# A third buffer for transposed features, and the selection of half 1 between the first gram products

## What is computed

```python
e = jnp.stack([tbl_0[ids[:, 0]], ..., tbl_26[ids[:, 26]]], axis=1)      # 2048 x 27 x 128
interactions = jnp.einsum('bfd,bgd->bfg', e, e).reshape(B, F * F)
x = interactions[:, TRIL_IDX]                                           # 351 pairs
z = jnp.concatenate([bottom_mlp_out, x], axis=1)
h = jnp.concatenate([z, bottom_mlp_out], axis=1)
h = jnp.maximum(h @ W_top1 + b_top1, 0.0)                               # 607 x 512
h = jnp.maximum(h @ W_top2 + b_top2, 0.0)                               # 512 x 256
y = h @ W_top3                                                          # 256 x 1
```

## Time and profile before

| | us |
|---|---|
| timed, median of three (lowest, highest) | 381.1 (380.89, 382.53) |
| profiled execution, span | 633.3 |
| TensorE matmul busy in it | 402.0 |
| GpSimd busy | 262.1 |
| VectorE busy | 254.0 |
| ScalarE busy | 144.4 |

### The profile page before, as it was taken

How to read it: one execution, slowest core, us unless ns; L and a number is a source line. 1 busy time by engine, 2 the same in 40 slices (tenths; PEclk the granted TensorE clock), 3 DMA queues, 4 the chain that set the end, 5 groups by cost and what they waited for, 6 DMA issues and landing times.

```text
span 633.3 us, 10256 instructions
## 1 busy us (share of the span) xinstructions
PE 402.0 (63%) x4321; PEld 374.0 (59%) x4321; DVE 254.0 (40%) x341; ACT 144.4 (23%) x268; POOL 262.1 (41%) x283
## 2 busy tenths in 40 slices
PE   2207655492738928298465956469392892839997
PEld 2206543492727918197464955469381992829986
DVE  3117955191315704074040921338040560407422
ACT  3204722020302213112311123012130221311521
POOL 6761447317370364505463073712646045550010
PEclk9999967597668969599595996769776896959999
DMA  8812652114221232114121241211321132211021
GB/s 200 174 50 77 175 167 77 52 28 135 55 55 40 64 104 65 41 40 128 35 75 28 45 134 47 61 39 36 127 64 53 36 81 84 64 40 39 9 61 9
DMA packets 44889, 45.76 MB, mean 72 GB/s; under 512 B 32720, under 2 KB 35558, under 8 KB 43948
## 3 DMA queue, kind: packets, MB, share of 16 engines
q1 hardware_dynamic: 33646, 26.52, 16.3%
q0 software_dynamic: 8896, 17.89, 10.9%
q10 hardware_dynamic: 2302, 0.70, 0.5%
HBM read 39.52 MB, written 5.55 MB: 71 GB/s over the span
## 4 chain that ended last, share of the span: by engine, by line
PE 50%; issue 20%; another core or an unknown queue 18%; ACT 5%; DVE 4%; DMA 2%; SPq 0%; ACTq 0%; DVEq 0%
PE work L389 21%; PE gram L416 16%; PE work L401 3%; PE work L442 2%; PE work L443 2%; PE work L444 2%; DVE onehot L536 2%; ACT embT L506 2%; ACT embT L675 2%; DMA inter<-in_tbl 1%; PE work L470 1%; DVE tab_lo L521 1%; DMA misc<-in_bottom 1%; PE work L459 1%
## 5 line engine op out<-in xcount | busy, mean ns | idle before, releaser
L359 POOL DMA_INDIRECT emb<-in_tbl,ids_all x272 | 258.2, 949 | 304.9 <-PE work L401 217.7
L536 DVE TENSOR_TENSOR onehot<-ids_bc,row_idf 125x1024 fp32r<-125x1024 int32 (+2 forms) x232 | 199.4, 921 | 94.0 <-PE work L389 60.9
L416 PE MATMUL gram<-embT 128*54 128x52 f32 x2048 | 110.3, 264 | 161.7 <-issue 134.6
L389 PE MATMUL work<-onehot,tab_hi 125*128 125x256 f32 x672 | 172.8, 296 | 51.2 <-DVE onehot L536 26.0
L416 PEld LDWEIGHTS gram<-embT 128*54 128x54 f32 x2048 | 93.9, 179 | 181.5 <-issue 164.2
L389 PE MATMUL work<-onehot,tab_lo 125*128 125x256 f32 x672 | 169.2, 291 | 0.0
L389 PEld LDWEIGHTS work<-onehot,tab_hi 125*128 125x128 f32 x672 | 133.8, 199 | 57.0 <-DVE onehot L536 32.4
L389 PEld LDWEIGHTS work<-onehot,tab_lo 125*128 125x128 f32 x672 | 134.3, 200 | 0.0
L675 ACT COPY embT<-work 128x512 f32<-128x512 f32 (+1 forms) x41 | 30.4, 795 | 163.5 <-PE work L389 98.9
L569 DVE SCALAR_TENSOR_TENSOR x_lo<-work,x_hi 128x512 fp32r<-128x512 f32 x16 | 11.0, 691 | 103.9 <-ACT x_hi L708 72.6
L683 ACT COPY inter<-gram 118x416 f32<-118x416 f32 x64 | 32.3, 506 | 66.5 <-remote 33.6
(11 more groups left out here) (56 smaller groups left out, 220.9 us busy)
## 6 DMA issues: line engine op xcount, KB each, us to landing
ids_bc<-in_sel_ids SPq DMA_DIRECT2D x7, 1280.0 KB
grams<-inter SPq DMA_DIRECT2D x64, 84.5 KB
emb<-in_tbl,ids_all POOLq DMA_INDIRECT x272
misc<-in_tbl SPq DMA_DIRECT2D x3, 448.0 KB
inter<-in_tbl SPq DMA_DIRECT2D x3, 448.0 KB
ids_bc<-in_sel_ids SPq DMA_DIRECT2D x4, 256.0 KB, 5.2
misc<-in_bottom SPq DMA_DIRECT2D x8, 128.0 KB
raw_hi<-in_tbl SPq DMA_DIRECT2D x1, 560.0 KB
```

Of the source, the lines that this page charges most:

```text
L359: pool.indirect_dma_start(out=emb[:, t % TILE_SLOTS, f, :], out_offset=None, in_=gather_tables[f], in_offset=bass.IndirectOffsetOnAxis(ap= ...
L389: mm = nc.tensor.matmul(out, part[0:k, CHUNK_AT[f] + c, :], onehot[0:k, at % RING, i * HALF:(i + 1) * HALF], start=(c == 0 and i % 2 == 0 ...
L416: last = nc.tensor.matmul(gram[side * SIDE:side * SIDE + TWO * NF, n % 2, q, 0:COLS], two.rearrange("d s f -> d (s f)"), two[:, :, 0:NG], ...
L536: nc.vector.tensor_tensor(onehot[0:k, at % RING, 0:width], ids_bc[0:k, four[0]:four[-1] + 1, :].rearrange("p i n -> p (i n)"), row_idf[0:k ...
```

## The change

- **A third slot.** embT_third, in the place of x_hi, x_lo and h2, holds tile 2; tile 3 uses slot 0. So the selection of half 1 can be copied (in two halves of a copy, one for each tile) while tile 1's slot is still in use.
- **Order of halves 0 and 1.** In half 0 the transposes of tile 0 come one set earlier where they can, and those of tile 1 behind sets 4 and 5, all copied by ScalarE. Then products 0, set 0 of half 1, products 1, transposes of tile 2, sets 1 and 2, products 2, bottom rows of half 0, transposes of tile 3, mlp1 of half 0, products 3, bottom rows of half 1. From half 2 on the order is that of before.
- **Weights.** They are all loaded by SyncE, after the last split of a table, into the place where their rest part will stand; ScalarE rounds them, VectorE subtracts in place, behind the one-hot 12 of half 1. On ScalarE the roundings stand behind the copies of tile 2.
- **Ids** for the selection come in a load for each set with a semaphore each. The row of ones sits directly under the pairs; VectorE fills 32 rows with ones before the packs of half 0 are loaded, and SyncE waits for that.

```diff
-    ONES = -(-PAIR_ROWS[-1] // QS) * QS
+    ONES = PAIR_ROWS[-1]
-        return range(j - 1, NGR if j == len(TWOS) - 1 else j) if 0 < j <= NGR else range(0)
+        return range(0)
+
+    FIRST_ROWS = [[], [(0, 0)], [(0, 1), (0, 2)], [(0, 3), (0, 4)], [(1, 0), (1, 1)], [(1, 2), (1, 3), (1, 4)]]
...
+    for j in range(len(TWOS)):
+        take_select(0, j)
+        for t, g in FIRST_ROWS[j]:
+            take_rows(t, [g])
+    take_gram(0)
+    take_gram(1)
+    take_select(1, 0)
+    take_rows(2)
+    take_select(1, 1)
+    take_select(1, 2)
+    take_gram(2)
+    take("bottom", 0)
+    take_rows(3)
+    take_gram(3)
+    take_mlp(0, "mlp1")
+    take("bottom", 1)
...
+        with nc.sbuf_tensor("embT_third", [P, P, NF], F32) as embT_third:
+            pass
+        with (nc.sbuf_tensor("raw_x", [P, 2, M1 + 2, HALF], F32), nc.sbuf_tensor("raw_h2", [P, M2, HALF], F32), nc.sbuf_tensor("raw_w1", [P, 2, CH + 1, H1], F32) as raw_w1,
+              nc.sbuf_tensor("raw_w2", [P, 2, M1, H2], F32) as raw_w2):
+            pass
...
-        w1_bot = [packed[:, 0:2, :].rearrange("p c n -> p (c n)"), h2[:, :, :].rearrange("p m n -> p (m n)")]
-        w1_raw = [stage[3][:, c * H1:(c + 1) * H1] for c in range(2)] + [w1_bot[1]]
-        w2_raw = stage[2][:, 0:M1 * H2]
+
+        def tile_embT(t):
+            return embT_third if t == 2 else embT[:, 0 if t == 3 else t % 2, :, :]
...
-            raw_last = max(n for n, to in enumerate(STAGE_OF) if to > 1)
-            sp.wait_ge(table_hi, raw_last + 1)
-            sp.wait_ge(table_lo, SPLIT_BY[raw_last])
-            for c in range(2):
-                sp.dma_start(w1_raw[c], w_top1[D + c * P:D + (c + 1) * P, :]).then_inc(w1_loaded[c], 16)
-            sp.dma_start(w2_raw.rearrange("p (c n) -> p c n", n=H2), w_top2.rearrange("(c p) n -> p c n", p=P)).then_inc(w2_loaded, 16)
-            sp.wait_ge(table_hi, NSEL)
-            sp.wait_ge(table_lo, len(PIECES))
-            sp.dma_start(bot[:, :, :], bottom_v[0]).then_inc(bot_loaded, 16)
-            sp.wait_ge(w1_padded, 1)
-            sp.dma_start(w1_raw[2][0:PAIR_ROWS[2], :], w_top1[D + 2 * P:D + PAIRS, :]).then_inc(w1_loaded[2], 16)
-            sp.dma_start(w1_raw[2][ONES:ONES + 1, :], b_top1.rearrange("(o n) -> o n", o=1)).then_inc(w1_loaded[2], 16)
+            def load_ids(h, j):
+                four = FOURS[j][0]
+                some = slice(four[0], four[-1] + 1)
+                sp.dma_start(ids_bc[:, some, :], sel_ids[h][:, some, :].to_broadcast([P, len(four), HALF])).then_inc(ids_bc_loaded[j], 16)
+
+            def load_weights():
+
+                for c in X_ORDER:
+                    if c == CH:
+                        sp.dma_start(raw_w1[:, 1, CH, :], w_top1[0:D, :]).then_inc(w1_loaded[CH], 16)
+                        sp.dma_start(raw_w1[:, 0, CH, :], w_top1[D + PAIRS:, :]).then_inc(w1_loaded[CH], 16)
+                    else:
+                        sp.dma_start(raw_w1[0:PAIR_ROWS[c], 1, c, :], w_top1[D + c * P:D + c * P + PAIR_ROWS[c], :]).then_inc(w1_loaded[c], 16)
+                    if c == CH - 1:
+                        sp.dma_start(raw_w1[ONES:ONES + 1, 1, c, :], b_top1.rearrange("(o n) -> o n", o=1)).then_inc(w1_loaded[c], 16)
+                sp.dma_start(raw_w2[:, 1, :, :], w_top2.rearrange("(c p) n -> p c n", p=P)).then_inc(w2_loaded, 16)
...
+            for j, (four, _, _) in enumerate(FOURS):
+                sp.wait_ge(onehot_ready, max(n for n, (two, _) in enumerate(ONEHOTS[0]) if SETS[0][two][0][0] in four) + 1)
+                load_ids(1, j)
+            sp.wait_ge(table_hi, NSEL)
+            sp.wait_ge(table_lo, len(PIECES))
+            sp.dma_start(bot[:, :, :], bottom_v[0]).then_inc(bot_loaded, 16)
+            load_weights()
             for h in range(HALVES):
-                if h + 1 < HALVES:
+                if 0 < h < HALVES - 1:
                     sp.wait_ge(onehot_ready, OH_AT[h + 1])
-                    sp.dma_start(ids_bc[:, :, :], sel_ids[h + 1].to_broadcast([P, NSEL, HALF])).then_inc(ids_bc_loaded, 16)
+                    for j in range(len(FOURS)):
+                        load_ids(h + 1, j)
                 store(2 * h)
                 if 2 * h + 2 == TILES - ID_SLOTS:
 
                     is_filled(sp, "rows", 2 * h + 1, NGR - 1)
                     sp.dma_start(ids_all[:, 0:2 * h + 2, :], ids_v[:, ID_SLOTS:, :]).then_inc(ids_loaded[2], 16)
-                if h + 1 < HALVES:
-                    is_filled(sp, "bottom", h)
-                    sp.dma_start(bot[:, :, :], bottom_v[h + 1]).then_inc(bot_loaded, 16)
+                if 0 < h < HALVES - 1:
+                    n = h if h > 1 else 0
+                    is_filled(sp, "bottom", n)
+                    sp.dma_start(bot[:, :, :], bottom_v[n + 1]).then_inc(bot_loaded, 16)
                 store(2 * h + 1)
+                if h == 1:
+                    is_filled(sp, "bottom", 1)
+                    sp.dma_start(bot[:, :, :], bottom_v[2]).then_inc(bot_loaded, 16)
                 if h:
                     sp.wait_ge(packed_split, CH * h)
+                else:
+                    sp.wait_ge(ones_ready, 1)
                 load_packs(sp, h, PACKS if h + 1 < HALVES else SP_PACKS, packs_loaded)
...
 
             pe.wait_ge(ident_ready, 1)
-            for h in range(HALVES):
-                for j in range(len(SETS[h])):
+            for j in range(len(TWOS)):
+                select(0, j)
+                for t, g in FIRST_ROWS[j]:
+                    rows(t, [g])
+            products(0, range(GRAMS))
+            select(1, 0)
+            products(1, range(GRAMS))
+            rows(2, range(NGR))
+            select(1, 1)
+            select(1, 2)
+            products(2, range(GRAMS))
+            bottom_rows(0)
+            rows(3, range(NGR))
+            mlp1(0)
+            products(3, range(GRAMS))
+            bottom_rows(1)
+            for h in range(2, HALVES):
+                for j in range(len(FOURS)):
                     select(h, j)
                     rows(2 * h, rows_behind(h, j))
-                    if j == bottom_behind(h):
-                        bottom_rows(h)
-                if h > 1:
-                    mlp2(h - 2)
+                bottom_rows(h)
+                mlp2(h - 2)
                 products(2 * h, range(GRAMS))
-                if h > 1:
-                    mlp3(h - 2)
+                mlp3(h - 2)
                 rows(2 * h + 1, range(NGR))
-                if 0 < h < HALVES - 1:
+                if h < HALVES - 1:
                     mlp1(h - 1)
                 products(2 * h + 1, range(GRAMS))
...
-                elif n == 0:
-                    dve.wait_ge(ids_bc_loaded, 16 * h)
+                elif h and c == 0:
+                    dve.wait_ge(ids_bc_loaded[j], 16 * h)
...
-            def split_w1_bottom():
-                dve.wait_ge(w1_bot_loaded, 32)
-                nc.vector.tensor_tensor(w1_bot[0], w1_bot[0], w1_bot[1], ALU.add).then_inc(w1_bot_summed, 1)
-                dve.wait_ge(w1_bot_summed, 1)
-                dve.memset(w1_bot[1][ONES - QS:ONES + 1, :], 0.0).then_inc(w1_padded, 1)
-                dve.memset(packed[ONES - QS:ONES, CH - 1, :], 0.0).then_inc(ones_zeroed, 1)
-                dve.memset(packed[ONES:ONES + 1, CH - 1, :], 1.0).then_inc(ones_ready, 1)
-                nc.vector.tensor_copy(w1_hi[:, CH, :], w1_bot[0]).then_inc(w1_hi_ready, 1)
-                dve.wait_ge(w1_hi_ready, 1)
-                nc.vector.tensor_tensor(w1_lo[:, CH, :], w1_bot[0], w1_hi[:, CH, :].bitcast(F32), ALU.subtract).then_inc(w1_split, 1)
-
             def split_w1(c):
                 k = X_ROWS[c]
-                dve.wait_ge(w1_loaded[c], 32 if c == 2 else 16)
-                nc.vector.tensor_copy(w1_hi[0:k, c, :], w1_raw[c][0:k, :]).then_inc(w1_hi_ready, 1)
-                dve.wait_ge(w1_hi_ready, c + 2)
-                nc.vector.tensor_tensor(w1_lo[0:k, c, :], w1_raw[c][0:k, :], w1_hi[0:k, c, :].bitcast(F32), ALU.subtract).then_inc(w1_split, 1)
+                if c == CH:
+                    dve.wait_ge(w1_loaded[c], 32)
+                    nc.vector.tensor_tensor(raw_w1[:, 1, c, :], raw_w1[:, 1, c, :], raw_w1[:, 0, c, :], ALU.add).then_inc(w1_bot_summed, 1)
+                dve.wait_ge(w1_hi_ready, X_ORDER.index(c) + 1)
+                nc.vector.tensor_tensor(w1_lo[0:k, c, :], raw_w1[0:k, 1, c, :], w1_hi[0:k, c, :].bitcast(F32), ALU.subtract).then_inc(w1_split, 1)
 
             def split_w2():
-                dve.wait_ge(w2_loaded, 16)
-                nc.vector.tensor_copy(w2_hi[:, :, :].rearrange("p c n -> p (c n)"), w2_raw).then_inc(w2_hi_ready, 1)
                 dve.wait_ge(w2_hi_ready, 1)
-                nc.vector.tensor_tensor(w2_lo[:, :, :].rearrange("p c n -> p (c n)"), w2_raw,
+                nc.vector.tensor_tensor(w2_lo[:, :, :].rearrange("p c n -> p (c n)"), raw_w2[:, 1, :, :].rearrange("p c n -> p (c n)"),
```

(96 more changed lines are left out.)

117 lines of the change are left out of this document (44 added, 73 removed).

## The result

| | kernel before | changed kernel |
|---|---|---|
| timed, median (lowest to highest) | 381.2 (380.89 to 382.53) | 378.94 (378.05 to 379.7) |
| profiled execution, time and span | span 380.0 (a second trace, below) | time 379.7, span 377.9 |
| start of half 2's selection | 113.34 | 111.21 |
| TensorE matmul busy | 343.6 (90%) | 341.6 (90%) |

A forecast was written before the change was run, and what follows sets the result against it. TensorE was taken to bind, GpSimd close behind. Half 2 starting at 138.8 instead of 140.8 gains 2.0 us, a faster clock in the first products 0.5: 381.1 - 2.5 = 378.6, range 374.5 to 384.5.

The forecast's parts named there:

- What binds: Whole kernel: TensorE binds by the rebuild at 383.3, GpSimd's gathers close behind at 375.5.
- The rebuilt scale: Timed run rebuilt from the undisturbed last half: half 2 at 111.3, 42.2 us a half, 383.3 in all.
- S = 29.5: Start of the disturbed trace: TensorE's standstill during the first gathers; all later times are shifted by 25.6 to 30 us.
- Steps 1 and 2: Half 1 up to its first products: 0.5 us lost by delayed splits, then products start 3.8 us sooner after selection.
- The clock: First products: less idle before them lets some matmuls run at 2.4 instead of 1.2 GHz; 0.5 us of at most 1.4.
- Step 3: Half 1's set 0 between products 0 and 1: 64 matmuls at 0.1216, from 91.8 to 99.7, covering the wait.
- hidden by 6: Weights' seven loads leave SyncE from 82.8, take 11 us, and VectorE asks at 100: no cost.
- Step 4: Weights' split on VectorE before one-hot 13 of half 1: TensorE waits 2.5 us, selection ends 3.7 us later.
- Step 5: Products 2 to half 2, 123.4 to 138.3; pack loads wait for the ones but stay hidden by 1.3 us.
- A: Rival, chance 0.25: GpSimd's gathers bind, early transposes of tile 1 remove its start idle, giving 375.5.
- B: Rival, chance 0.25: the stall of the weights' split eats the gain, half 2 starts where it did: 381.
- C: Rival, chance 0.15: pack loads behind VectorE's late split delay tile 3's copies and products 3: 384.5.

The follow-up runs named there:

- the two kernels that shortened TensorE's chain: Changed kernel with VectorE's splits, all but the sum, behind half 1's one-hots: 379.35; changed kernel with the weights' loads behind the store of tile 0: 379.66.
- The kernel with one part alone: Kernel before with only the bottom rows of half 0 moved behind the products of tile 0: 381.0, ratio 0.9977.
- the three with moved splits: Changed kernel with sum and splits behind half 1's one-hots: 379.92; that with one gather fewer per tile 2 to 15: ratio 0.9961; only splits behind: 379.35.
- the one with a part undone: Changed kernel with the transposes of tile 1 behind the products of tile 0 again, all copied by ScalarE: 379.46, ratio 0.9928.
- the last four kernels above: Changed kernel, weights' loads later and splits last: ratio 0.9962; with lightened gathers, two calls: 0.9615, 0.9645; kernel before with lightened gathers: 0.9743.
- the kernel with both moves: Changed kernel with the weights' loads behind the store of tile 0 and VectorE's splits, all but the sum, behind half 1's one-hots: ratio 0.9962.

## Why the prediction was right

The forecast was 378.6 and the time 378.94, and the sign, the place and the binding engine were right. The sum was less good than that: several of its terms were off and cancelled. By its steps, with the second trace of before:

- **What binds.** TensorE, with GpSimd close behind: confirmed by one gather fewer (no change), and by the two kernels that shortened TensorE's chain and ran into the gathers at once. "About 2 for the last to land" measured 1.95 (2.25 with the weights' loads moved), the last gather "at 344" ends at 344.6 in the changed kernel. GpSimd's idle in before, "between 0 and 4", was 0.4 + 1.4 = 1.8 us beyond its usual 0.3 and cost nothing: its last gather ends at 345.71, and TensorE comes to the transposes of tile 15 at 348.95.
- **The rebuilt scale.** S = 29.5 put the first products at 61.3, they were at 61.83. Half 2 of before was rebuilt at 111.3 and stood at 113.34: two costs were missing, 1.1 us in the selection (16.66 for 15.56) and 0.6 us up to the end of products 1 (73.31, rebuilt to 72.7). The other way, 42.2 us a half was 1.1 too much: measured are 205.7/5 = 41.1. The last half's 36.46 holds a wait of 1.1 us for ScalarE's copies (605.36 against the end of the transposes), and in halves 2 to 6 layer 1 stands between and hides it. I had added layer 1 and kept the wait. 5 x 1.1 - 2.0 = 3.5 us is, but for 0.2, the 3.3 us by which 383.3 lay above the span of 380.0.
- **Steps 1 and 2.** First products 3.8 us earlier (less 0.5 for step 1): 5.35 in the two traces, 4.4 against the mean of the five other kernels with this start (56.93 to 58.30). Right in kind; the size moves by a microsecond from run to run.
- **The clock.** 0.5 taken of a possible 1.4; it was 1.35. But the prediction's reason for it, a shorter idle before the products, is not what decided. In before the granted clock has fallen from 1.00 to 0.50 by 52 us, while TensorE is in the selection and busy for 1.05 to 1.18 of each 2 us, long before it stands for 3.43 us. The kernel with one part alone has that stand no more, and its products take 5.02 us at a clock of 0.50 all the same. In the changed kernel the transposes of tile 1 stand among the last sets, and the clock is 1.00 throughout from 44 to 60 us; with these transposes put back it is 0.50 and the products take 4.98 us.
- **Step 3.** Set 0 at 7.9 us (64 x 0.1216 = 7.8): 12.1 with the stop, 4.2 us lost, of which 1.5 are the fall of the clock behind it, which three other kernels with the stop don't have. This term is missing from the prediction. I had costed the weights' loads "hidden by 6" by asking when VectorE needs them, not whom their traffic stops.
- **Step 4.** TensorE's wait at one-hot 13 "2.5": 2.12. One-hots and selection from the end of tile 2's transposes to the end of the third set "105.7 to 122.1", 16.4: from 77.7 to 94.0, 16.3. The price of the block, 3.7: moving the splits behind the one-hots got 3.6 back, 3.5 to 3.9 from the end of set 0 on.
- **Step 5.** From products 2 to half 2, 14.9 us: 16.3. Layer 1 waits for a row of handovers, rounding of the bottom, three splits and VectorE's copies, which I had counted as done by then. Of the packs the forecast was right: they leave SyncE from 83.35, behind the fill with ones at 83.01, the last at 96.2, and ScalarE reads them at 99.11 without a wait.

So the changed kernel's half 2, foreseen at 108.8 (138.8 - 29.5 - 0.5), came at 111.21, 2.4 us late: 1.5 and 0.9 won at the first products, 4.2 and 1.4 lost in set 0 and behind products 2, the rest small. The kernel before had its half 2 2.0 us later than rebuilt. The two misses cancel in the difference; the forecast of 2.5 owes its closeness to that. It is luck, and the size of each miss hangs on one execution: with a gather fewer the same program on TensorE had half 2 at 109.66, 0.9 us late instead of 2.4.

**The rivals.** A needed GpSimd to bind: it does not, but it is 1.8 us away (the last four transposes start at 348.3, the last gather is there by 344.6 + 1.95 = 346.5). B was that the stall eats the gain; the stall was of its forecast size, and a loss of B's kind came from the stop in set 0 instead. C's packs stayed hidden.

The Trainium skill's gap of 109 ns for 256 columns ("TensorE: Matmul & The Clock Gate", Back-to-back issue gap) was weighed against 121.6 ns in a disturbed trace. In the undisturbed one 128 matmuls take 15.55 us at full granted clock, 121.5 ns each: the measurement decides against the 109 ns, and A's support from it is gone. The section gives that formula for a matmul by itself; for a stream of weight loads and matmuls, which this is, it has 81 ns at 128 columns and 131 ns at 512, and 121.5 ns at 256 lies between these. The prediction left that out.

## What to carry to other kernels

When two engines' chains lie within two microseconds of each other, a saving on the first can be worth no more than the distance to the second: the two best single moves here brought half 2 forward by 3.6 and 4.2 us and the end by nothing that could be timed. Ask of each transfer that is moved not only who needs it and when, but what else runs at that moment: here a burst of loads that nobody waited for went with a stop of TensorE. And before a wait is taken off one engine, follow what its other partner has queued behind the same handover. Before a microsecond is read from two traces, look at how two traces with the same work on the binding engine differ: here by 1.5 us.

## What the runs showed of the hardware

**A burst of loads goes with a stop of TensorE.** It stood for 2.27 to 2.55 us, each time before the sixth matmul of set 0, in all five kernels that load the weights right before the first products and start set 0 right behind them (the changed kernel, the one with a gather fewer, and the three with moved splits), and not at all in the one with later loads or in the one with a part undone, where set 0 comes 4.7 us later and has 319 GB/s beside it. In that stretch the DMA view of the changed kernel (60 to 64 us) holds one packet of the queue that loads instructions:

```profile
q1 hardware_dynamic: 655, 0.94, 83.3%
q0 software_dynamic: 116, 0.24, 20.6%
q8 instruction: 1, 0.02, 1.9%
```

The packets of this queue bear out that TensorE waited for this one. In the five kernels with the stop the packet starts 3.9 to 4.2 us behind the start of products 0, 0 to 0.35 us before TensorE stops; with later loads it starts 1.5 us behind it. So under the burst it is 2.3 to 2.7 us late, and the stop is 2.27 to 2.55 long. In all five the sixth matmul of set 0 starts 2.5 to 2.6 us after the packet does. In the two kernels without a stop TensorE comes to that matmul, in the normal course of its work, 2.5 us after the packet: with later loads since the packet was early, with a part undone since 17 transposes stand ahead of set 0. The packets also keep step with TensorE's program: the ninth starts behind 2294 of its matmuls and weight loads in each of three kernels looked at, and there are 34 packets for 8642 of these. This is the likely cause and fits all seven traces; it is not shown, since the trace names no releaser and does not say whose instructions a packet holds. The Trainium skill ("Runtime: NRT & Kernel Launch", Terms) says that an engine's instruction memory is refilled in blocks of 16 KiB; the 34 packets with 0.56 MB on the profile's page agree, 16.5 KB each.

**The same kernel at 381 and at 634 us.** A span like the 633.3 us of the first trace of before needs no profiler, as I had allowed for: the last four kernels above, and the kernel before beside them, took 606 to 638 us in all executions, with a profile or without, and a chip on which the kernel before took 381.6 gave 634.5 some minutes later. TensorE then stands, with nothing that releases it, mostly while GpSimd gathers. The waits of the kernel with both moves (span 630.9), as in the earlier trace rows:

```profile
PEld gram L469 <- issue: 138.8, 115, 7.8
ACT x_hi L779 <- remote: 109.8, 11, 20.4
```

There one gather fewer in 14 tiles takes 16.6 us off the kernel before (634.1 to 617.5) and 22.2 off the one with both moves (632.4 to 610.3), against the 17.5 us that these gathers last: the time follows the gathers, where at 381 us they cost nothing. In both conditions TensorE stops without a releaser while much is loaded; whether it is the same mechanism is open, and so is what sets the condition.
